# Cosines taken by DVE from the projection bank, keys summed by POOL, and values of a block merged in 65 columns of one bank

## The reference

```python
q = rope(ln(x) @ Wq + bq);  k = rope(ln(ctx) @ Wk + bk);  v = ln(ctx) @ Wv + bv
rope(z) = z * cos + rotate(z) * sin
attn = softmax(where(valid, q @ k.T / 8, -inf));  out = (attn @ v) @ Wo + bo
```

## Time and profile before

| | |
|---|---|
| time, median of 3 runs | 1414.58 us (1409.71 to 1415.38) |
| the profiled execution, its own time | 1410.14 us |
| its span | 1408.3 us |
| mean granted clock of PE, of 2.4 GHz | 0.913 |
| preparation, to the first projection | 0 to 57 us |
| attention, first pair's projections alone | 57 to 100 us |
| attention | 100 to 1016 us |
| output projection and routing | 1016 to 1175 us |
| experts and output | 1175 to 1408 us |

### The profile page before, as it was taken

One profiled execution on the slowest core, in us unless ns is written; L12 is line 12 of the kernel. 1 busy time (PEld: TensorE's weight loads), 2 busy tenths in 40 slices (PEclk: granted clock), 3 DMA queues, 4 the chain that ended last, 5 costly groups with the idle time before them and its releaser, 6 DMA issues. The chain is left out here.

```text
span 1408.3 us, 31670 instructions
## 1 busy us (share of the span) xinstructions
PE 1110.8 (79%) x10244; PEld 725.9 (52%) x10407; DVE 1053.9 (75%) x1791; ACT 650.8 (46%) x1196; POOL 689.2 (49%) x496
## 2 busy tenths in 40 slices
PE   1658888889889888888898987999778615999953
PEld 0324555556556555555555654666467503656631
DVE  6647997998899799899899989999558622444424
ACT  3425555555546555555554555566455401322310
POOL 0053854864664485485466458555556561000052
PEclk9758999999999999999999999999989758999985
DMA  7042124221521512422142151220097122111133
GB/s 241 20 115 82 36 52 118 49 57 32 136 50 23 139 35 52 108 60 59 33 132 50 23 139 37 54 68 13 19 348 270 41 97 76 56 53 55 57 91 107
DMA packets 99015, 115.58 MB, mean 82 GB/s; under 512 B 45197, under 2 KB 79054, under 8 KB 98638
## 3 DMA queue, kind: packets, MB, share of 16 engines
q1 hardware_dynamic: 88270, 86.92, 22.8%
q10 hardware_dynamic: 7552, 18.51, 4.0%
q0 software_dynamic: 3072, 8.39, 1.9%
HBM read 43.61 MB, written 30.80 MB: 53 GB/s over the span
## 5 line engine op out<-in xcount | busy, mean ns | idle before, releaser
L800 DVE TENSOR_REDUCE part_max<-mx 128x1 f32<-128x427 f32 x768 | 419.6, 592 | 73.6 <-PE mx L583 72.7
L708 ACT ACTIVATE prob<-sc 128x512 f32<-128x512 f32 x640 | 348.9, 595 | 227.2 <-PE sc L571 223.8
L887 POOL TENSOR_TENSOR prob_lo<-prob 128x1024 bf16<-128x1024 f32 x128 | 251.3, 1963 | 267.6 <-ACT prob L708 267.5
L583 PE MATMUL mx<-K,Q 128*128 128x427 bf16 x768 | 243.3, 358 | 83.7 <-DVE part_max L800 54.4
L609 PE MATMUL pv<-VV,prob 128*128 128x129 bf16 x2560 | 275.6, 224 | 1.8 <-POOL prob_lo L887 1.6
L611 PE MATMUL pv<-VV,prob_lo 128*128 128x65 bf16 x2560 | 266.6, 196 | 0.0
L812 DVE TENSOR_TENSOR prob_lo<-prob 128x1024 bf16<-128x1024 f32 x192 | 253.9, 1322 | 6.2 <-ACT prob L708 6.1
L571 PE MATMUL sc<-Q,K 65*128 65x512 bf16 x640 | 251.1, 392 | 9.5 <-issue 4.3
L609 PEld LDWEIGHTS pv<-VV,prob 128*128 128x128 bf16 x2560 | 237.8, 100 | 33.8 <-issue 3.5
L611 PEld LDWEIGHTS pv<-VV,prob_lo 128*128 128x128 bf16 x2560 | 232.8, 100 | 27.1 <-issue 2.9
L570 PE MATMUL sc<-Q,K 128*128 128x512 bf16 x519 | 203.7, 393 | 0.5 <-ACT prob L708 0.5
(11 more groups left out here) (186 smaller groups left out, 1885.0 us busy)
## 6 DMA issues: line engine op xcount, KB each, us to landing
we<-in_w_exp ACTq DMA_DIRECT2D x16, 768.0 KB, 6.2
q32s<-q SPq DMA_DIRECT2D x128, 64.0 KB, 2.0
Q<-next_q_hi SPq DMA_DIRECT2D x32, 256.0 KB, 3.6
attention_out<-o_out SPq DMA_DIRECT2D x64, 128.0 KB, 2.0
o_in<-attention_out SPq DMA_DIRECT2D x16, 512.0 KB, 6.0
expert_inputs<-zeros SPq DMA_DIRECT2D x7, 768.0 KB, 5.2
expert_outputs<-zeros SPq DMA_DIRECT2D x7, 768.0 KB, 6.5
VV<-next_v SPq DMA_DIRECT2D x16, 322.5 KB, 3.8
```

What stands on the lines that cost most here:

```text
L583: ins = pe.matmul(mx[:, bank, 0:pl.width], Q1[a][:, c * QC + qt * P:c * QC + (qt + 1) * P], K1[a][:, k0:k0 + pl.width], start=True, stop=True)
L708: act.activation(prob[:, s % PRING, j, :], sc[n % 2][:], ACT.Exp, scale=HD ** -0.5).then_inc(exp_done, 1)
L800: dve.tensor_reduce(part_max[:, b_ % 2, qt, h:h + 1], mx[:, pl.part_banks(qt, h)[0]:pl.part_banks(qt, h)[-1] + 1, 0:pl.width], mybir.AxisL ...
L887: pool.tensor_tensor(prob_lo[:, s % PRING, 0:g, :], prob[:, s % PRING, 0:g, :], hi_half(prob[:, s % PRING, 0:g, :])[:, :, 1::2], ALU.subtr ...
```

## The change

Three things change, all in `attend`:

- Cosines: the product reads the projection in PSUM: one fused operation of DVE adds the bias and multiplies (`cosines`). It stands in the slot after the projection and no longer at the next hook, and `by_cos` has two buffers. ACT still copies the projection to `q32`, for the rotation. The next projection now waits for the cosines (`cos_done`) where it waited for ACT (`pj_read_act`).
- For the key units POOL adds cosines and sines (`sums`), and DVE only puts in the first key, which a one-column addition makes (`first_key`). Query units are added by DVE as before.
- In `times_v` all three products of a quarter are added up in the same 65 columns: high half with the 65 columns of high values and ones, high half with the 64 columns of low values, low half with the 65. A block takes 260 columns of one bank, blocks alternate between the two banks of `pv`, ACT copies 260 columns and not 516, and POOL's sum (line 899) is gone.

The core of the diff (waits of other engines that only follow from it are left out):

```diff
-                            need(pe, pj_read_act, pair, QK_UNITS, u, least)
+                            need(pe, cos_done, pair, QK_UNITS, u, least)
...
-                                at = (qt % 2) * VW
-                                pe.matmul(pv[:, qt // 2, at:at + VW], hi[:, 2 * qt * P + 1:2 * (qt + 1) * P:2], VV[a][:, t, :],
-                                          start=t == 0 and qt % 2 == 0, stop=False, skip_group_check=True)
-                                ins = pe.matmul(pv[:, qt // 2, at + HD:at + VW], prob_lo[:, s % PRING, j, qt * P:(qt + 1) * P],
-                                                VV[a][:, t, HD:VW], start=False, stop=t == pl.kt - 1, skip_group_check=True)
+                                out = pv[:, i % 2, qt * (HD + 1):(qt + 1) * (HD + 1)]
+                                hi_q = hi[:, 2 * qt * P + 1:2 * (qt + 1) * P:2]
+                                pe.matmul(out, hi_q, VV[a][:, t, HD:VW], start=t == 0 and qt == 0, stop=False, skip_group_check=True)
+                                pe.matmul(out[:, 0:HD], hi_q, VV[a][:, t, 0:HD], start=False, stop=False, skip_group_check=True)
+                                ins = pe.matmul(out, prob_lo[:, s % PRING, j, qt * P:(qt + 1) * P], VV[a][:, t, HD:VW],
+                                                start=False, stop=t == pl.kt - 1, skip_group_check=True)
...
-                        need(act, turn_done, pair, QK_UNITS, u - 3, least)
...
-                        act.activation(o_raw[:, i % 2, :, :].rearrange("p (b t) v -> p b t v", b=2),
-                                       pv[:, :, 0:2 * VW].rearrange("p b (t v) -> p b t v", t=2), ACT.Copy).then_inc(o_copied, 1)
+                        act.activation(o_raw[:, i % 2, :, :].rearrange("p t v -> p (t v)"), pv[:, i % 2, 0:QT * (HD + 1)],
+                                       ACT.Copy).then_inc(o_copied, 1)
...
-                        need(dve, turn_done, pair, QK_UNITS, u, least)
-                        dve.tensor_tensor(by_cos[:, 0:n], q32[:, u % 4, 0:n], (ropeq, ropek)[kind][:, 0, cols], ALU.mult).then_inc(cos_done, 1)
+                        dve.sem_inc(cos_seen, 1)
+                        need(dve, turn_done, pair, QK_UNITS, u - 1, least)
+                        dve.scalar_tensor_tensor(out=by_cos[:, u % 2, 0:n], in0=pj[:, 0:n], scalar=bqk[:, kind:kind + 1],
+                                                 in1=(ropeq, ropek)[kind][:, 0, cols], op0=ALU.add, op1=ALU.mult).then_inc(cos_done, 1)
+                    def first_key(pair, least=0):
...
+                        dve.tensor_tensor(key0[:], by_cos[:, 0, 0:1], by_sin[:, 0:1], ALU.add).then_inc(key0_made, 1)
...
-                        need(dve, sin_done, pair, QK_UNITS, u + 1, least)
+                        if kind == 0:
+                            need(dve, cos_done, pair, QK_UNITS, u + 1, least)
+                            need(dve, sin_done, pair, QK_UNITS, u + 1, least)
+                            need(dve, qk_lo_made, pair, QK_UNITS, u - 1, least)
+                            dve.tensor_tensor(turned[:, u % 2, 0:n], by_cos[:, u % 2, 0:n], by_sin[:, 0:n], ALU.add).then_inc(turn_done, 1)
+                            return
+                        need(dve, sum_made, pair, 4, u - 4 + 1, least)
+                        need(dve, key0_made, pair, 1, 1, least)
                         need(dve, qk_lo_made, pair, QK_UNITS, u - 1, least)
-                        if kind == 0:
-                            dve.tensor_tensor(turned[:, u % 2, 0:n], by_cos[:, 0:n], by_sin[:, 0:n], ALU.add).then_inc(turn_done, 1)
-                            return
-                        dve.tensor_tensor(turned_raw[:, 0:n], by_cos[:, 0:n], by_sin[:, 0:n], ALU.add).then_inc(raw_done, 1)
-                        need(dve, raw_done, pair, 4, u - 4 + 1, least)
-                        if u == 4:
-                            dve.tensor_copy(key0[:], turned_raw[:, 0:1]).then_inc(key0_made, 1)
-                            need(dve, key0_made, pair, 1, 1, least)
                         dve.scalar_tensor_tensor(out=turned[:, u % 2, 0:n], in0=invalid[:, cols], scalar=key0[:, 0:1],
                                                  in1=turned_raw[:, 0:n], op0=ALU.mult, op1=ALU.add).then_inc(turn_done, 1)
...
                         for s in range(LAG, BLOCKS * pl.groups + LAG):
                             slot(p, s, last)
                             if not last:
-                                for k in range(pl.units + 2):
-                                    if s == pl.hook_slot(k):
-                                        hooks(p + 1, k, 1)
-                                    if s == pl.hook_slot(k) + 1 and 0 <= k - 1 < QK_UNITS:
-                                        turn(p + 1, k - 1, 1)
...
+                                for u in range(QK_UNITS):
+                                    if s == pl.hook_slot(u) + 1:
+                                        cosines(p + 1, u, 1)
+                                for u in range(QK_UNITS):
+                                    if u == 4 and s == pl.hook_slot(u + 1) + 1:
+                                        first_key(p + 1, 1)
+                                    if s == pl.hook_slot(u + 1) + 1:
+                                        turn(p + 1, u, 1)
...
+                    def sums(pair, u, least=0):
+                        kind, cols, n = pl.unit_block(u)
+                        need(pool, sin_done, pair, QK_UNITS, u + 1, least)
+                        pool.sem_inc(sum_seen, 1)
+                        need(pool, cos_done, pair, QK_UNITS, u + 1, least)
+                        pool.tensor_tensor(turned_raw[:, 0:n], by_cos[:, u % 2, 0:n], by_sin[:, 0:n], ALU.add).then_inc(sum_made, 1)
...
+                        if 4 <= k - 1 < QK_UNITS:
+                            sums(pair, k - 1, least)
...
-                        pool.tensor_tensor(o_sum[:], o_raw[:, i % 2, :, 0:HD], o_raw[:, i % 2, :, HD:2 * HD], ALU.add).then_inc(o_summed, 1)
```

42 lines of the change are left out of this document (22 added, 20 removed).

## The result

| | before | after |
|---|---|---|
| median of 4 runs, us | 1412.14 (1409.31 to 1415.38) | 1380.13 (1375.83 to 1384.52) |
| profiled execution, us | 1410.1 | 1384.5 |
| its span, us | 1408.3 | 1382.7 |

A forecast was written before the change was run, and what follows sets the result against it. DVE was taken to bound the first four blocks, with PE and DVE evenly matched in free ones; 8.0 us a pair over seven pairs gave 56 us less, forecast 1356, own range 1345 to 1368, wide range 1337 to 1391.

The forecast's parts named there:

- three cases at 1386 to 1389: Rivals: projection waits for cosines (1386), key turn waits for POOL (1389), fused cosines slowed (1388); chance 0.23 together.
- Part 1: Cosines on DVE: eight operations per pair fall to 740 and 541 ns, 6.4 us a pair less.
- The rival by which they are slowed in the loop: Fused cosines on DVE slowed like the old ones; only 3.75 us a pair and the end remain: 1388, chance 0.04.
- All comes back: Rival: all 10.2 us a pair shed by DVE is gained and PE keeps its full clock: 1340, chance 0.12.
- Part 2: Key additions moved from DVE to POOL: 3.75 us a pair off DVE; the one-column addition costs nothing.
- The forecast's 1.3 us for pieces that meet: Chosen deduction per pair for pieces of PE and DVE meeting in the blocks: gain 9.3 becomes 8.0 us.
- The fifth stretch: Fifth block of a turn: 14.01 less 0.94 us gives 13.1 us.
- Part 3: Three value products a quarter on PE: 2 ns more each, 5 us in all, of which 1 us is counted.
- The case on the other side: Rival: the third value product costs PE 43 ns, so PE becomes the bound: about 1435, chance 0.07.
- The first pair: Preparation ahead of the loop: slower on PE, faster on POOL's chain, 5.67 us of DVE waiting behind; zero, 3 us either way.
- the projection waits for the cosines: Rival: PE's next projection waits about 1 us in each of four odd units a pair: 1386, chance 0.12.
- the key turn waits for POOL: Rival: POOL's 1.1 us sum ends the key chain in full, returning 4 x 1.1 us a pair: about 1389, chance 0.07.

The follow-up runs named there:

- the four products: Changed kernel with the product of the low values done twice in each quarter, so values are wrong by that part: 1.0090 of the kernel before.
- the keys back: Changed kernel with DVE again adding cosines and sines of the key units and copying the first key, without POOL's key sums: 0.9728 of the kernel before.
- the values back: Changed kernel with two value products a quarter, 516 columns copied and POOL's sum again, as in the kernel before: 0.9734 of the kernel before.

## Why the prediction was right in sign and short in size

The time fell into the stated range, but partly by luck. The range went up to 1391 to take in three cases at 1386 to 1389 that the loop does not show; what filled the room were causes that no case named. The prediction's own signs speak against its size: "wrong if the turn is above 113 us, or if free blocks grow". One of six turns took 113.4 us (mean 112.4), and free blocks grew by 0.15.

**Part 1: right.** 746 and 529 ns, 6.4 us a pair off DVE; the first two stretches, which it rules, came out within 0.3 us, and with the cosines from SBUF 2.0 of 2.2 points go. The rival by which they are slowed in the loop fell: the fused cosines took 740 to 752 and 518 to 544 ns in the loop, every one of them. In "All comes back" the full clock came true (the lower level fell from 65 to 27 us over the loop, and the 0.89 and 0.92 of rows 2 are 1.00 after), and its 1340 us did not.

**Part 2: the step that failed.** "The copy of one column becomes an addition of one column: nothing." It is 1.72 us: in the loop this addition of one column, with two SBUF inputs, lasted until POOL's operation ended. The prediction used this contention for the operations removed and not for those put in or left: fused key operations on DVE went from 728 to 1048 ns and low halves from 1319 to 1400. By the groups 4.8 us of 10.2 came back; by the stretches the first five gained 5.7 us a pair where the count had 9.3. Taking the additions away shows 2.2 us a pair of it directly (16.33 to 14.76, 13.79 to 13.18), to within 0.1 and 0.3 us of the forecast. The forecast's 1.3 us for pieces that meet was the only term for it, where 3.6 were missing. The low halves lengthened for two reasons, which the runs separate. They take 1304 ns with the cosines alone, 1331 with the keys' part added, 1363 with the merged values added, 1400 with both and 1363 with both and the key copied: 59 ns, 1.4 us a pair, go with the values' part, which no term of the forecast had, and 27 to 37 ns, up to 0.9 us a pair, with the keys' part.

**The fifth stretch: mis-sized.** 0.94 us was taken off as if DVE had the last word. The 0.56 us addition in it is shorter than that mean, its fused operation grew by 0.47, and behind both stands a wait of PE for the values' low half (1.09 before, 0.92 after), which a floor made of busy time cannot show. Moving that one operation gave 12.7, below the 13.1 of the forecast.

**Part 3: right about PE.** Three products go in 92 ns against 86, and a free block takes 0.15 us more; forecast were 2 ns a quarter and free blocks as before, so the term was too small by a factor of three, and small either way. The case on the other side (43 ns for the third product) fell, since it has 29 ns and the quarter 6 more in all. Its price is borne out by the four products: 28 ns a quarter do cost over 3 points; only its condition was not met. As a whole the merged values are worth -0.4 (intervals overlap), 0.7 and 0.5 points in the three pairs of kernels that differ by them, and 0.4, 1.3 and 1.3 us in the first seven stretches of a turn.

**The first pair: outside its 3 us.** It got 4.8 us later (0 forecast), with a granted clock from 57 to 100 us that was about the same (0.58 before, 0.62 after). Its cover, the 5.67 us wait before the first reduction, is the end of the same chain and covers nothing. The rivals "the projection waits for the cosines" and "the key turn waits for POOL" came true here, where PE waits 1.6 to 2.7 us a unit for the cosines (0.6 to 0.8 for ACT before; some 1.5 was forecast), and not in the loop.

**The jump stretch: not forecast, partly open.** It grew by 0.9 us in the mean, 5.5 over the kernel. Where the clock falls after the jump, one window before (start to end; columns of the earlier trace rows):

```profile
701.00:705.00 4.00, 3.48 (x22) 2.03 (x22) 1.32 (x3) 1.19 (x2) 0.18 (x1) 0.57 0.67 152
```

and after:

```profile
681.00:685.00 4.00, 4.00 (x34) 2.39 (x33) 2.39 (x4) 1.29 (x3) 0.00 (x0) 0.50 0.99 207
```

The granted clock is 0.57 of the full 2.4 GHz in one and 0.50, the lower level of 1.2 GHz, in the other, in both behind an idle PE at the jump (3.3 us before, 3.4 after); in the next 4 us the changed kernel has 0.77, the one before 1.00. With the same instructions from turn to turn, the stretch goes with the time at the lower level. In the profile after, it takes 17.5 us with none of it, 17.8 and 17.9 with 3.4 us, and 18.9, 19.0 and 19.4 with 6.8 us; in the one before, 16.3 with none and 17.1 to 18.1 with 3.4. Why the lower level lasts longer after is open. The merged values alone do not explain it: kernels with the values as before have means of 17.2, 18.0 and 18.3 us, those with three products 17.7 to 18.6.

**The sum as it came.** From stretch to stretch in the two profiles, over the loop: the first five gain 10.0, 9.7, 4.6, 14.2 and 1.4 us, the free one loses 1, the jump 5.5; together 33.3. Less 4.8 for the first pair, 28.5; the profiled executions differ by 25.6 and the medians by 32.0, and the part behind the last reciprocal took 394.0 us before, 396.9 after, and 395.7 to 398.5 in the other runs on such chips, where no edit touches it. The forecast had 56: the first five stretches alone fell 25 us short of their 65, of which its 1.3 us a pair for pieces that meet covered 9.

## What to carry to other kernels

Count for each operation that is moved between DVE and POOL what it does to the other engine's operations with two SBUF inputs, not only its own time; such an operation on DVE can cost the rest of a POOL operation even at one column. Take operands from PSUM where they are there anyway: that gain was whole. When two engines are within half a microsecond of each other, look for the order within a slot (who waits for the second of two operations): one swap took 1.1 us off a turn, though the total moved by no more than the noise. And compare granted clocks before calling a difference in one stage an effect: the same program reached its first reciprocal at 129.5 and at 133.8 us.

## What the runs showed of the hardware

- An addition of one column on DVE took 0.16 us in the first pair, while POOL was between operations, and in the loop 0.15 us after the end of a POOL operation; begun beside one it took 0.48, 1.05, 1.72 and 1.85 us in different kernels, and ended within 0.02 us of POOL's operation.
- The fused operation with PSUM and one SBUF operand had means of 742 to 747 ns for 512 columns and 527 to 536 for 320 in the loops of eleven kernels, whatever POOL did. The same operation with both tensors in SBUF had means of 610 to 1443 ns for 320.
- POOL's operations lengthen too: sines of 320 columns took 0.86 us in the first pair and 1.85 in the third stretch after. Their mean in the loop was 1165 ns before, 1354 with the keys back, 1353 with the values back and 1599 after.
- Products of 64 and 65 columns, each with a weight load of its own, follow each other at 29 ns, and at 33 or 34 between two of 65 columns; the weight load does not show.
